# A mixture-of-experts' second product as three fp32r products of halves, with another order of the last tiles

## What is computed

```python
x = x + tanh(g_xattn) * attention(layernorm(x), ctx, ctx, mask, wq, wk, wv, wo)   # 32 query heads, 8 kv heads of 128, rope
n = layernorm(x)
logits = einsum('bsd,ed->bse', n, route_w)                  # 8 experts
topk_v, topk_idx = top_k(logits, 1)
weight = one_hot(topk_idx) * topk_v
h = einsum('bsd,erd->bser', n, A)                           # rank 16
wh = weight[..., None] * h
out = einsum('bser,eor->bso', wh, Bw)                       # the second product: 128 (expert, rank) pairs -> 512
x = x + tanh(g_ffn) * out
```

## Time and profile before

| | before |
|---|---|
| median of 3 runs | 1104.44 us (1104.04 to 1106.16) |
| profiled execution, its time | 1103.77 us |
| its span in the trace | 1101.4 us |
| PE busy | 99% |
| DVE busy | 80% |
| granted PE clock | 0.998 |

### The profile page before, as it was taken

How to read it: one execution, slowest core, us unless ns; L and a number is a source line. 1 busy time by engine, 2 the same in 40 slices (tenths; PEclk the granted TensorE clock), 3 DMA queues, 4 the chain that set the end, 5 groups by cost and what they waited for, 6 DMA issues and landing times.

```text
span 1101.4 us, 16992 instructions
## 1 busy us (share of the span) xinstructions
PE 1088.9 (99%) x5628; PEld 918.4 (83%) x5628; DVE 882.0 (80%) x1410; ACT 642.3 (58%) x1111; POOL 593.1 (54%) x518
## 2 busy tenths in 40 slices
PE   9999999999999999999999999999999999999998
PEld 7888888778888888888888888888888888888886
DVE  7876757888888888888887998777777777777887
ACT  7563466675666666666656544555555555555543
POOL 5552488787777777777754333333333333333423
PEclk9999999999999999999999999999999999999999
DMA  7859973595546464646389546453535353533202
GB/s 258 265 209 350 375 251 142 178 382 167 202 162 210 154 210 155 210 154 210 136 305 375 178 135 222 141 194 114 187 114 185 114 185 107 182 106 115 67 11 77
DMA packets 106085, 206.26 MB, mean 187 GB/s; under 512 B 8848, under 2 KB 58640, under 8 KB 100112
## 3 DMA queue, kind: packets, MB, share of 16 engines
q1 hardware_dynamic: 105712, 204.79, 54.9%
q10 hardware_dynamic: 288, 0.39, 0.1%
HBM read 122.31 MB, written 82.84 MB: 186 GB/s over the span
## 4 chain that ended last, share of the span: by engine, by line
PE 85%; issue 4%; DVE 4%; POOL 3%; SPq 2%; DMA 1%; ACT 1%; DVEq 0%; POOLq 0%; ACTq 0%
PE attn L924 30%; PE proj L858 28%; PE score L875 10%; PE attn L820 4%; PE attn L909 3%; PE attn L911 3%; PE turned L886 2%; PE score L820 2%; PE turned L820 2%; DMA v_kept<-vst 1%; SPq L560 1%; PE small L975 1%; SPq L584 1%; POOL rstd L1730 1%; POOL rot L1784 0%
## 5 line engine op out<-in xcount | busy, mean ns | idle before, releaser
L924 PE MATMUL attn<-wo_s,o_s 128*128 128x512 f32 x1524 | 374.8, 395 | 0.0
L858 PE MATMUL proj<-xB,wq_s 128*128 128x512 f32 x1344 | 335.0, 392 | 0.0
L924 PEld LDWEIGHTS attn<-wo_s,o_s 128*128 128x128 f32 x1524 | 280.8, 188 | 56.9 <-DVE o_s L1234 0.2
L858 PEld LDWEIGHTS proj<-xB,wq_s 128*128 128x128 f32 x1344 | 252.8, 189 | 53.1 <-issue 1.9
L1784 POOL TENSOR_TENSOR rot<-rot,tab 128x512 f32<-128x512 f32 x110 | 161.3, 1466 | 149.2 <-ACT rot L1527 149.0
L1572 ACT ACTIVATE o_s<-attn 128x512 fp32r<-128x512 f32 x127 | 69.4, 595 | 120.0 <-PE attn L911 120.0
L875 PEld LDWEIGHTS score<-k_r,q_r 128*128 128x128 f32 x1024 | 123.9, 191 | 7.9 <-issue 1.9
L1141 DVE TENSOR_TENSOR q_r<-q_r,tab 128x512 f32<-128x512 f32 x128 | 123.9, 968 | 1.5 <-ACT x_third L1527 1.4
L875 PE MATMUL score<-k_r,q_r 128*128 128x64 f32 x1024 | 121.3, 271 | 0.8 <-DVE prob_even L1207 0.8
L1226 DVE TENSOR_TENSOR p_low<-turned,p_high 64x512 fp32r<-64x512 f32 x128 | 87.9, 687 | 17.1 <-ACT p_high L1564 14.8
L1548 ACT ACTIVATE copies<-proj 128x512 f32<-128x512 f32 x96 | 57.5, 599 | 74.3 <-PE proj L858 74.1
(11 more groups left out here) (250 smaller groups left out, 1649.3 us busy)
## 6 DMA issues: line engine op xcount, KB each, us to landing
wq_kept<-wq_s SPq DMA_DIRECT2D x16, 1792.0 KB, 6.3
wq_s<-wq_kept SPq DMA_DIRECT2D x16, 1792.0 KB, 8.4
v_kept<-vst SPq DMA_DIRECT2D x64, 256.0 KB, 4.3
v_s<-v_kept SPq DMA_DIRECT2D x128, 128.0 KB, 4.9
wo_kept<-wo_s SPq DMA_DIRECT2D x32, 512.0 KB, 4.9
wo_s<-wo_kept SPq DMA_DIRECT2D x32, 512.0 KB, 5.4
k_kept<-kst SPq DMA_DIRECT2D x32, 256.0 KB, 2.4
wq_raw<-in_wq SPq DMA_DIRECT2D x16, 512.0 KB, 8.4
```

The source lines that it names most:

```text
L858: last = e.matmul(dst[:, :], wq_s[:, b % 2, A, s, kt, :], xB[:, B, mv, kt, :], start=(first and kt == 0 and m == 0), stop=(kt == 1 and m = ...
L924: last = e.matmul(out_bank(k, bp)[:, :], o_s[:, s, bp, h, :], wo_s[n % WO_SLOTS][:, m, :], start=(h == 0 and i == 0), stop=(h == GROUP - 1 ...
```

## The change

- The second product. lora_bT is split into halves once (lora_s): ACT copies the high half at the end of step 29, POOL subtracts the low half at the end of its step 29 (behind the inverse deviations of norms_of(29)). ACT's copy of a tile's turned weights is now the high half (turned_s, fp32r), and a new DVE instruction per tile subtracts it from the bank to make the low half (weighted_low). PE makes three fp32r products for two fp32 passes, with 512 columns, or twice three with 256 for the last tile. Where the mix overwrites the bank that holds the turned weights, it waits for the low half first; elsewhere only the third product waits for it.
- Orders in the steps 30 to 33. DVE makes "turn weighted" at place 6, which now stands ahead of add_out(k - 1, 1). ACT's place 6 stands ahead of its shifts of the middle ropes.
- The end. PE mixes tile 11 (a1) between route b1 and turn c1, and mixes the rest in the old order; its turning of the weights of 12 stands ahead of route c1. ACT scales a1 right behind its copy of c1. DVE has the new subtractions between the routings. Tile 13 (b1), which DVE added and SP stored, is now scaled by ACT, added by POOL and stored by a DMA that ACT issues at its end.
- The four counts of the routing's steps on DVE become one.

The diff, without the lines that only rename semaphores:

```diff
--- before.py
+++ after.py
@@ -341,7 +341,10 @@
         expert_s = sb_at(base + 126976, "expert_s", [P, 2, DM])
 
         last_s = sb_at(2048, "last_s", [P, 4, DM])
-        mix_s = sb_at(2048 + 16384, "mix_s", [P, 5, DM])
+
+        turned_s = [sb_at(start + 2048 * i + 4 * ER, f"turned_s{n}_{i}", [P, 2, P], F32R)
+                    for n, (start, tiles) in enumerate(((base + 126976, 2), (base + 122880, 2), (2048, 4))) for i in range(tiles)]
+        mix_s = sb_at(2048 + 16384, "mix_s", [P, 6, DM])
         far_raw = [sb_at(base + place, f"far_raw{i}", [P, KT, 512]) for i, place in enumerate((135168, 122880))]
         cursor = [base + 143360]
 
@@ -351,6 +354,8 @@
             return sb_at(offset, name, shape, dt)
 
         x_near = sb_at(cursor[0], "x_near", [P, 2 * CHUNKS, 512])
+
+        lora_s = sb_at(cursor[0], "lora_s", [P, 2, DM], F32R)
         raw = sb("raw", [P, RAW, 512])
         warm = sb_at(cursor[0], "warm", [P, 512], F32R)
         v_both = sb("v_both", [P, 2, CHUNK_TILES, DH], F32R)
...
@@ -499,6 +505,12 @@
             if t >= HALF_TILES + 4:
                 return last_s[:, t - HALF_TILES - 4, :]
             return (expert_s if t < HALF_TILES + 2 else late_s)[:, t % 2, :]
+
+        def expert_turned(t):
+
+            if t >= HALF_TILES + 4:
+                return turned_s[4 + t - HALF_TILES - 4]
+            return turned_s[(0 if t < HALF_TILES + 2 else 2) + t % 2]
 
         def out_bank(k, bp):
 
@@ -652,12 +664,12 @@
                 elif n < TILES - 3:
                     e.wait_ge(out_ready_g, n - HALF_TILES + 1)
                 elif n < TILES - 1:
-                    e.wait_ge(out_ready, n + 1 - (HALF_TILES - 3))
+                    e.wait_ge(out_ready, n + 1 - (HALF_TILES - 2))
                 if n < TILES - 1:
                     e.dma_start(out_tiles[n], acc[:, t, :]).then_inc(stored[t], 16)
                 else:
                     for i, cols in enumerate(LAST_PARTS):
-                        e.wait_ge(out_ready, HALF_TILES + 3 + i)
+                        e.wait_ge(out_ready, HALF_TILES + 2 + i)
                         e.dma_start(out_tiles[n][:, cols], acc[:, t, cols]).then_inc(stored[t], 16)
                 if half + 1 < HALVES:
                     e.wait_ge(stored[t], 16)
@@ -774,7 +786,8 @@
                     if 30 + t // 2 == k - 1:
                         store(t)
             for t in range(HALF_TILES, TILES):
-                store(t)
+                if t != TILES - 3:
+                    store(t)
             for t in range(HALF_TILES):
                 e.wait_ge(stored[t], 32 if t + 1 < HALF_TILES else 48)
 
@@ -965,19 +978,26 @@
                     e.wait_ge(weighted, t + 1)
                     turn(b_work, 0, at[:, 0:ER]).then_inc(weighted_turned, 1)
                     if par and t < HALF_TILES:
-                        drained[score.name] = weighted_copied, t + 1
+                        drained[score.name] = weighted_low, t + 1
                 else:
                     b = small if t < HALF_TILES else b_work
-                    e.wait_ge(weighted_copied, t + 1)
+                    if t == 0:
+                        e.wait_ge(lora_low, 1)
+                    e.wait_ge(weighted_high, t + 1)
                     if par and t < HALF_TILES:
                         e.wait_ge(out_ready, t)
-                    if t + 1 < TILES:
-                        e.matmul(b[:, :], at[:, ER:ER + P], lora_bT[:, :], start=True, stop=True).then_inc(mixed, 1)
-                    else:
+                    if t + 1 == TILES:
 
                         e.wait_ge(mix_scaled, 3)
-                        for b_part, cols in zip((turned, b), LAST_PARTS):
-                            e.matmul(b_part[:, cols], at[:, ER:ER + P], lora_bT[:, cols], start=True, stop=True).then_inc(mixed, 1)
+                    for b_part, cols in ((b, slice(0, DM)),) if t + 1 < TILES else zip((turned, b), LAST_PARTS):
+                        if b_part.name == b_work.name:
+
+                            e.wait_ge(weighted_low, t + 1)
+                        for i, (s, m) in enumerate(SPLIT_PRODUCTS):
+                            if s:
+                                e.wait_ge(weighted_low, t + 1)
+                            last = e.matmul(b_part[:, cols], expert_turned(t)[:, s], lora_s[:, m, cols], start=(i == 0), stop=(i == 2))
+                        last.then_inc(mixed, 1)
 
             def experts(what, k):
                 for t in tiles_of(k):
@@ -1083,12 +1103,12 @@
             expert("turn", c0)
             expert("route", b0)
             expert("route", b1)
+            expert("mix", a1)
             expert("turn", c1)
             expert("route", c0)
+            expert("turn weighted", b0)
             expert("route", c1)
-            expert("turn weighted", b0)
             expert("turn weighted", b1)
-            expert("mix", a1)
             expert("mix", b0)
             expert("turn weighted", c0)
             expert("mix", b1)
@@ -1269,20 +1289,24 @@
                 logits = b[:, 0:EXPERTS]
                 if what == "route":
                     e.wait_ge(routed, t + 1)
-                    e.tensor_reduce(best, logits, AX.X, ALU.max).then_inc(top_found, 1)
-                    e.wait_ge(top_found, t + 1)
+                    e.tensor_reduce(best, logits, AX.X, ALU.max).then_inc(routing, 1)
+                    e.wait_ge(routing, 4 * t + 1)
                     e.scalar_tensor_tensor(out=ranks, in0=logits, scalar=best, in1=tab[:, RANKS:RANKS + EXPERTS],
-                                           op0=ALU.is_equal, op1=ALU.mult).then_inc(top_ranked, 1)
-                    e.wait_ge(top_ranked, t + 1)
-                    e.tensor_reduce(rank, ranks, AX.X, ALU.max).then_inc(rank_found, 1)
-                    e.wait_ge(rank_found, t + 1)
+                                           op0=ALU.is_equal, op1=ALU.mult).then_inc(routing, 1)
+                    e.wait_ge(routing, 4 * t + 2)
+                    e.tensor_reduce(rank, ranks, AX.X, ALU.max).then_inc(routing, 1)
+                    e.wait_ge(routing, 4 * t + 3)
                     e.scalar_tensor_tensor(out=weight, in0=ranks, scalar=rank, in1=best.to_broadcast([P, EXPERTS]),
-                                           op0=ALU.is_equal, op1=ALU.mult).then_inc(weight_set, 1)
-                    e.wait_ge(weight_set, t + 1)
+                                           op0=ALU.is_equal, op1=ALU.mult).then_inc(routing, 1)
+                    e.wait_ge(routing, 4 * t + 4)
                     by_expert = "p (e r) -> p e r"
                     e.tensor_tensor(at[:, 0:ER].rearrange(by_expert, e=EXPERTS),
                                     b[:, EXPERTS:ROUTED].rearrange(by_expert, e=EXPERTS),
                                     weight.unsqueeze(2).to_broadcast([P, EXPERTS, RANK]), ALU.mult).then_inc(weighted, 1)
+                elif what == "turn weighted":
+                    high, low = (expert_turned(t)[:, part] for part in range(2))
+                    e.wait_ge(weighted_high, t + 1)
+                    e.tensor_tensor(low, b[:, 0:P], high.bitcast(F32), ALU.subtract).then_inc(weighted_low, 1)
                 elif what == "mix":
                     here, src = acc[:, t % HALF_TILES, :], small if t < HALF_TILES else b
                     if t + 1 < TILES:
@@ -1388,10 +1412,10 @@
                     q_add(*q)
                 prob_low(k, *((0, 1) if k % 4 == 3 else (1,)))
                 between(k, 5)
+                between(k, 6)
                 add_out(k - 1, 1)
                 if k == 1:
                     ropes_left(0)
-                between(k, 6)
                 between(k, 7)
                 between(k, 8)
                 expert_norms_begin(norms_of(k))
@@ -1438,6 +1462,7 @@
             prob_low(k + 3, 0, 1)
             expert_norms_begin(tiles_of(k + 1)[1:])
             add_out(k + 2, 0)
+            experts("turn weighted", k)
             expert_norms_end(tiles_of(k + 1))
             add_out(k + 2, 1)
 
@@ -1448,6 +1473,7 @@
             expert_norms_end(tiles_of(k + 2))
             (b0, b1), (c0, c1) = tiles_of(k + 2), tiles_of(k + 3)
             add_out(k + 3, 0)
+            experts("turn weighted", k + 1)
             expert_norms_begin([c0])
             expert_norms_end([c0])
             add_out(k + 3, 1)
@@ -1455,9 +1481,12 @@
             expert_norms_end([c1])
             expert("route", b0)
             expert("route", b1)
+            expert("turn weighted", b0)
             expert("route", c0)
+            expert("turn weighted", b1)
             expert("route", c1)
-            expert("mix", b1)
+            expert("turn weighted", c0)
+            expert("turn weighted", c1)
             expert("mix", c0)
             expert("mix", c1)
 
@@ -1579,7 +1608,7 @@
                     e.activation(at, b_turn[:, :], ACT.Copy).then_inc(x1_copied, 1)
                 elif what == "turn weighted":
                     e.wait_ge(weighted_turned, t + 1)
```

(27 more changed lines are left out.)

## The result

The changed kernel takes 1105.31 us (median of 19 runs, 1104.30 to 1106.79), the kernel before 1103.90 in 19 runs beside it; the ratio is 1.0013 with an interval of 1.0007 to 1.0018. It is 1.4 us slower (0.8 to 2.0), less than the 2.2 us within which I called it the same. The forecast was 1105.2, from a kernel before of 1104.44: a difference of 0.75. So that the two times agree to 0.1 us is partly luck, since the kernel before ran 0.54 faster in these runs and the change cost about twice what I had.

A forecast was written before the change was run, and what follows sets the result against it. PE bounds the kernel (busy 1088.9 of 1101.4 us), with DVE nearly without slack in the changed stretches. First half +0.15 and end +0.6 sum to +0.75, from the median 1104.44 to 1105.2 us; range 1102.4 to 1107.2.

The forecast's parts named there:

- The product: PE's mixes: three fp32r products take 0.68 us against 0.86, giving 0.17 to 0.18 per tile, 2.8 if all counts.
- steps 31 and 33: First-stretch mixes that wait for DVE's new subtraction to read their bank; PE waits about 0.4 us each.
- The splitting of lora_bT: Steps 29 and 30: POOL's new subtraction delays DVE's normalisations, and PE's output product gets all 0.53 us (0 to 1.3).
- Steps 30 and 32: First-stretch mixes: PE loses its 0.2 us wait for ACT and gains 0.17; DVE's 1.2 idle hides the subtractions.
- The first stretch: First eight tiles through the experts, 616 to 690 us: 1.4 of shorter products and 0.4 of waits lost, +0.15.
- The middle: Up to the last output product: DVE's subtractions for tiles 8 and 9 delay normalisations, +0.42 us.
- The end: After the last output product: DVE's tile 13 routing ties with POOL's addition, POOL wins; last issue +0.6 in all.
- The signs: Expected in the profile: products 0.68 to 0.70, 690 us output within 0.5, PE idle 2 to 3 from 1092.
- (1): End: DVE, not POOL, wins the tie at tile 13's routing; end -0.35, sum -0.2, 1104.2 us; chance 0.33.
- (2): Faster: DVE's subtractions and the lock are hidden, PE keeps its gain; 3.1 us less, 1101.3; chance 0.08.
- (3): Slower: DVE bounds both stretches, its subtractions waiting for ACT's copy; up to 7.8, at half 1108.4 us; chance 0.12.
- (4): Mixes: fp32r products cost what fp32 passes did, no PE gain, +0.35 more at the end, 1105.6 us; chance 0.05.

The follow-up runs named there:

- e3_no_low_first: Changed kernel without DVE's subtraction for tiles 0 to 7, whose third product multiplies the high half again: 1103.29 us, ratio to the kernel before 0.9998.
- e4_orders_only: Changed kernel's orders, moved store and ACT copies with the kernel before's fp32 products, no halves or lora_bT splitting: 1102.53 us, ratio 0.9989.
- e1_route_psum: Changed kernel, but DVE's routing operation takes its second operand from PSUM (the logits): 1102.65 us, ratio to the kernel before 0.9994.
- e8_halves_end: Changed kernel with halves for tiles 8 to 15 alone, POOL's lora_bT subtraction later, routing operand from PSUM: 1102.79 us, ratio 0.9988.
- e10_turned_bank: Changed kernel, but the even mixes of tiles 0 to 7 go to bank turned instead of small: 1104.33 us, ratio 1.0002.

## Why the forecast held, and where it was off

**The product.** Right: three products took 0.69 to 0.71 us on the chain where nothing held them up. But behind a wait the chain gives them 0.93. I had no such term: from the end of the subtraction (648.41) to the end of the mix (649.49) pass 1.08 us, and I had 0.70. Of the 0.38, 0.15 lie between the subtraction and the mix. Of the other 0.23, 0.15 are the start of a group, which in a stream lies over its neighbour's last matmul, so that the chain doesn't count it, and 0.08 are a longer first matmul (0.93 in the list against 0.84 to 0.86). The first weight load begins 0.03 us ahead of the matmul there and 0.23 ahead where nothing waits (e3_no_low_first), which fits a load in the open; no run tests it by itself. This is the mis-sized term of the steps 31 and 33: each put PE back by 0.67 us, and I had 0.30 and 0.32.

**The splitting of lora_bT.** Right in kind, 0.37 for 0.53. PE met it one operation earlier than I had it, at the turning of the second tile that reads the normalised row, and not at the output product.

**Steps 30 and 32.** Right: the lost wait for ACT gives 0.2 each (e4_orders_only: 0.43 in all), and DVE's idle time, 0.48 and 0.38 us before the mix where it was 1.22, hides the subtractions.

**The first stretch.** +0.15 forecast, +0.59 measured. The sign and the mechanism held, the gain of the products is gone there as written. The 0.37 and 0.35 us more in the steps 31 and 33 make up 0.7; the smaller lora term took 0.17 back, and 0.1 went in PE's other waits.

**The middle.** +0.42 forecast, +0.40 measured: two subtractions of 0.21 on a DVE that has no gap. The 0.35 us of shorter mixes went into PE's wait for DVE as written. e4_orders_only has 0.39 less there with the same orders, so it is the halves.

**The end.** +0.18 forecast and +0.18 measured to the last issue, with the tie decided for POOL by 0.07 us, and the routing at 1.22 us. The steps in between came out too: with 2.56 us taken off (1.97 of start, 0.59 of first stretch) the routing of tile 13 ended at 1093.81 (1093.82 forecast), the last subtraction at 1097.46 (1097.45) and the last addition at 1099.28 (1099.17). The landing of the last store was the piece I left out: I added the old 2.56 us from the last issue to the end of the span, and it became 2.92. This and the start behind a wait are the main terms that make +1.53 of +0.75.

**The signs.** The groups of products, L1136 over 2 us beside POOL, the waits in steps 31 and 33 alone and the operation of tile 13 over 1 us are there. Three came out beyond what I had written. The two waits are 0.6 and not 0.4. The output product at 690 us is 0.59 later, with the start taken off, and not within 0.5; with the start left in, 2.56, which is over the 1 us that I had called wrong, but 1.97 of it lies ahead of the change. And from 1094.5 to 1101.0 PE idles for 1.05 us and not for 2 to 3; it is its weight loads that wait for DVE for 2.0.

**The rivals.** (1), the other way round of the tie: e1_route_psum takes away more than this lock (1.42 us at the end for my 0.95), since the one of tile 12 goes with it. (2), faster: e3_no_low_first shows that the gain in the first stretch is there once DVE does nothing for it (1.11 us under before, 1.3 forecast), and e8_halves_end that the 1.35 at the end is not there, even without the lock. (3), slower by 4 us: ACT's copy was never late for DVE in the first stretch (it ended at least 0.29 us before each subtraction), so DVE did not lose its queue. (4) is out by the 0.69 us.

## What to carry to other kernels

A product of halves takes work from PE and puts an instruction on the vector engine, and where that engine has no slack the shorter matmuls turn into waits: here the products were 2.7 us shorter in all (15 times 0.17, and 0.14 for the last tile, in which I had counted no gain), and still the halves cost 2.1 us in the end. With the lock, the splitting and the bank mended they were still no clear gain over the plain products. Look for who reads the bank that the product overwrites, and send the product elsewhere if the new reader is late in its queue. When a step is moved onto POOL or in time, look at which vector operations with both inputs in SBUF it will now meet; taking one input from PSUM, where the same value stood, was worth 1.9 us in the changed kernel, 1.1 with the orders alone and 0.9 in the one before.

## What was unexpected of the hardware

- A group of three matmuls behind a wait took 0.93 us from its start to its end, where one in a stream took 0.84 to 0.86 and the chain counts 0.69 of it (both waits, and also in e10_turned_bank, whatever the wait was for).
- The operation of eight columns, 0.23 us, was held up by a POOL addition that began 0.07 us before it, for the whole of it (1.22), and with one operand in PSUM not at all (0.22). A start listed a little earlier doesn't save it: at 1082.06, 0.04 us before POOL's addition, it took 1.35.
- With four stores issued within 0.9 us (1101.09 to 1101.98) the last 128 KB landed 2.5 us after its issue, against 2.0 without one of them.
